# Expert layer: first-layer weights taken in alternating order, with loads cut into quarters and issued by the landing of earlier ones

## What is computed

```python
logits = einsum('bntd,des->bntes', grouped, Wc) + bc            # after a layernorm
perm = (logits + tie == max over the 32 tokens of a group)      # one token per expert and group
permuted = einsum('bnesd,...', grouped, perm)                   # gather
inner = relu(einsum('bnesd,esdf->bnesf', permuted, W1) + b1)    # 512 -> 32 per expert
result = einsum('bnesf,esdf->bnesd', inner, W2) + b2            # 32 -> 512 per expert
out = x + tanh(g_ffn) * einsum('bnesd,bntes->bntd', result, perm)   # scatter back
```

## Time and profile before

| | us |
|---|---|
| median of 3 runs | 1812.2 (1804.32 to 1812.33) |
| the profiled execution, its own time | 1815.87 |
| its span (first to last instruction) | 1814.1 |
| first gather of batch 0 | 754.5 |
| one batch, batches 1 to 14 | 62.1 to 67.7 |

### The profile page before, as it was taken

The page is one execution under the profiler, slowest core; times in us unless marked ns, Lnnn a source line. Parts: engine busy times, 40 slices in busy tenths (PEclk is TensorE's granted clock), DMA queues, the critical chain, the costliest instruction groups (busy, mean ns, idle before and its releaser), DMA issues.

```text
span 1814.1 us, 53065 instructions
## 1 busy us (share of the span) xinstructions
PE 1666.4 (92%) x23192; PEld 1178.4 (65%) x23192; DVE 1341.6 (74%) x1980; ACT 819.0 (45%) x1070; POOL 615.7 (34%) x841
## 2 busy tenths in 40 slices
PE   7899999999999999889999899999989999998974
PEld 3677777777777777767656656665765676576551
DVE  6877777777777777547777867877787787678657
ACT  3433333333333333465465555556546555554631
POOL 3577777777777777111011001101100110110100
PEclk9999999999999999999999999999999999999987
DMA  7345555545454544265667567567657766765762
GB/s 261 124 141 176 153 177 163 165 152 164 153 175 155 186 152 178 104 234 201 210 245 263 188 226 274 185 239 261 236 190 252 269 205 218 267 205 206 245 226 78
DMA packets 135845, 358.35 MB, mean 198 GB/s; under 512 B 13760, under 2 KB 17600, under 8 KB 117952
## 3 DMA queue, kind: packets, MB, share of 16 engines
q1 hardware_dynamic: 124384, 273.16, 45.0%
q10 hardware_dynamic: 11232, 81.79, 12.5%
HBM read 286.75 MB, written 68.16 MB: 196 GB/s over the span
## 4 chain that ended last, share of the span: by engine, by line
PE 57%; DVE 15%; issue 10%; POOL 10%; ACT 6%; DMA 1%; SPq 0%; POOLq 0%; DVEq 0%; ACTq 0%
PE ps L1220 14%; PE ps L1192 8%; PE ps L1247 8%; PE ps L208 6%; PE ps L836 6%; POOL qc L478 4%; POOL qc L479 4%; PE ps L1262 4%; PE ps L194 4%; PE ps L1242 3%; DVE mx L604 2%; DVE qc L620 2%; DVE qs L621 2%; ACT gat L1068 2%; PE ps L799 2%
## 5 line engine op out<-in xcount | busy, mean ns | idle before, releaser
L176 POOL TENSOR_TENSOR b_va<-b_mv,eps_layer 128x2 f32<-128x2 f32 x64 | 12.5, 195 | 858.3 <-DVE b_mv L167 857.3
L1108 DVE STREAM_TRANSPOSE res<-res 128x2048 f32<-128x2048 f32 x128 | 292.0, 2294 | 0.1
L1063 ACT ACTIVATE gat<-ps 128x1536 f32<-128x1536 f32 (+1 forms) x128 | 172.2, 1345 | 218.0 <-PE ps L1192 218.0
L779 PE MATMUL ps<-xTh,qh 128*128 128x512 f32 x512 | 208.9, 408 | 6.2 <-DVE qs L621 2.1
L779 PE MATMUL ps<-xTh,ql 128*128 128x512 f32 x512 | 200.0, 391 | 0.0
L779 PE MATMUL ps<-xTl,qh 128*128 128x512 f32 x512 | 200.0, 391 | 0.0
L1131 DVE COPY res<-ps 128x1024 f32<-128x1024 f32 x128 | 156.7, 1224 | 51.0 <-PE ps L1247 51.0
L1073 ACT ACTIVATE res<-ps 128x1024 f32<-128x1024 f32 x128 | 131.2, 1025 | 105.6 <-PE ps L1247 105.6
L1192 PE MATMUL ps<-sel,xin 32*128 32x128 f32 x4096 | 155.3, 286 | 25.1 <-ACT sel L236 13.6
L1192 PEld LDWEIGHTS ps<-sel,xin 32*128 32x128 f32 x4096 | 131.1, 188 | 61.1 <-ACT gat L1063 40.2
L1114 DVE COPY gat<-ps 128x512 f32<-128x512 f32 (+1 forms) x128 | 103.9, 812 | 84.2 <-PE ps L1192 83.9
(11 more groups left out here) (126 smaller groups left out, 3175.0 us busy)
## 6 DMA issues: line engine op xcount, KB each, us to landing
gat<-in_W ACTq DMA_DIRECT2D x48, 1024.0 KB, 7.8
xT<-in_xT SPq DMA_DIRECT2D x32, 1024.0 KB, 5.9
xin<-in_x SPq DMA_DIRECT2D x64, 512.0 KB, 3.8
x_scratch<-xin SPq DMA_DIRECT2D x64, 512.0 KB, 3.4
xin<-x_scratch SPq DMA_DIRECT2D x64, 512.0 KB, 4.2
xin<-x_scratch SPq DMA_DIRECT2D x128, 256.0 KB, 5.5
out<-xin SPq DMA_DIRECT2D x128, 256.0 KB, 3.6
xT<-in_W SPq DMA_DIRECT2D x25, 1024.0 KB, 5.2
```

What stands on the lines that cost most here:

```text
L779: last = e.matmul(ps[:, 2 + n % 2, :], a[:, c, n * DH:(n + 1) * DH], b[:, c, :], start=(k == 0), stop=(k == len(parts) - 1))
L1063: e.activation(o, v, ACT.Copy).then_inc(m_gaA.sem, 1)
L1108: e.transpose(v, v).then_inc(m_tr.sem, 1)
```

## The change

W1 is taken in order 0 to 7 in even batches and 7 to 0 in odd ones (`piece`). Pieces 2, 4, 5 stay on chip. The two pieces that a batch uses last lie in the two ring buffers and are the first two of the next batch, so a batch loads two ring pieces (`load_end`) and piece 3 (`load_middle`), which has the place of the y tiles 0 to 3: three pieces instead of five. Each is loaded as four quarters of 256 KB (2 KB for a partition) with a semaphore each, and a quarter is issued when the one two before it has landed. All W1 loads are SyncE's; ScalarE keeps the three W2 loads. `load_x` is cut into eight tiles of 256 KB, tile t issued when tile t-2 has landed and gather 6 or 7 is done. `load_y` 0 to 3 waits until `inner` has used the middle piece. The places of the relu's output and of W2's last piece change sides with the batch.

```diff
-W1_KEPT = (1, 4, 6)
-W1_MOVED = (0, 2, 3, 5, 7)
+W1_KEPT = (2, 4, 5)
+W1_MIDDLE = 3
+QUARTERS = 4
...
+        def piece(i, p):
+            return p if i % 2 == 0 else 2 * C - 1 - p
...
-            def load_x(i, v):
-                e.wait_ge(m_gap.sem, m_gap.at(i - 1, 2 * (C - 1) + v // 2))
-                e.wait_ge(m_w1.sem, m_w1.at(i - 1, 4 + v))
-                route.load(e, i, v)
+            def load_end(i, k, c):
+                e.wait_ge(m_w1.sem, m_w1.at(i, k))
+                if c >= 2:
+                    e.wait_ge(d_ring[k][c - 2].sem, d_ring[k][c - 2].at(i + 1))
+                e.dma_start(quarter(ring[k], c), quarter(w1_dram[piece(i, 2 * C - 1 - k)], c)).then_inc(d_ring[k][c].sem, 16)
+            def load_middle(i, c):
+                if i:
+                    k = (i - 1) * NT - NY + c
+                    e.wait_ge(d_ys[c].sem, d_ys[c].at(k // NY))
+                    e.wait_ge(m_w2.sem, m_w2.at(i - 1, 5))
+                if c >= 2:
+                    e.wait_ge(d_mid[c - 2].sem, d_mid[c - 2].at(max(i - 1, 0)))
+                e.dma_start(quarter(middle, c), quarter(w1_dram[W1_MIDDLE], c)).then_inc(d_mid[c].sem, 16)
+            def load_x(i, t):
+                e.wait_ge(m_gap.sem, m_gap.at(i - 1, 2 * (C - 1) + t // TH))
+                if t >= 2:
+                    e.wait_ge(route.d_x[t - 2].sem, route.d_x[t - 2].at(i))
+                route.load(e, i, t)
             def load_y(b, t):
                 k = b * NT + t
+                if t < NY and live(b + 1):
+                    e.wait_ge(m_w1.sem, m_w1.at(b + 1, piece(b + 1, W1_MIDDLE)))
...
             for i in range(B + 1):
+                if live(i):
+                    if i != 1:
+                        for c in range(QUARTERS):
+                            load_middle(i, c)
+                    for k, c in ((0, 0), (0, 1), (1, 0), (1, 1), (1, 2), (1, 3), (0, 2), (0, 3)):
+                        load_end(i, k, c)
+                for t in range(0, NY, 2):
+                    if live(i + 1):
+                        load_x(i + 1, t)
+                        load_x(i + 1, t + 1)
+                    if live(i - 1):
+                        load_y(i - 1, t)
+                        load_y(i - 1, t + 1)
+                for t in range(NY):
+                    if live(i + 1):
+                        load_x(i + 1, NY + t)
+                    if live(i - 1):
+                        store_y(i - 1, t)
                 if live(i - 1):
-                    for t in range(NY):
-                        load_y(i - 1, t)
-                if live(i):
-                    for m in (2, 3, 4):
-                        load_first(e, i, m)
-                if live(i + 1):
-                    for v in range(NV):
-                        load_x(i + 1, v)
-                if live(i - 1):
-                    for t in range(NY):
-                        store_y(i - 1, t)
                     for t in range(NY, NT):
                         load_y(i - 1, t)
                     for t in range(NY, NT):
...
-                    if u in (1, 4):
-                        load_first(e, i + 1, u // 3)
...
-            def inner(i, n):
-                c = n // 2
-                if n in W1_MOVED:
-                    k = NM * i + W1_MOVED.index(n)
-                    e.wait_ge(d_ring[k % 2].sem, d_ring[k % 2].at(k // 2))
+            def inner(i, p):
+                n, c = piece(i, p), p // 2
                 for q in range(n % 2 * 16, n % 2 * 16 + 16):
+                    if q % 4 == 0 and n not in W1_KEPT:
+                        e.wait_ge(*landed(i, p, q % 16 // 4))
```

More of the change, by code:

```diff
@@ L86, in build @@
         ring = [xT[:].rearrange("p c t -> p (c t)"), xin[:, 3].rearrange("p n d -> p (n d)")]
-        d_ring = [Mark(top, nc, f"ring{k}", 1, 16) for k in range(2)]
+        d_ring = [[Mark(top, nc, f"ring{k}{c}", 1, 16) for c in range(QUARTERS)] for k in range(2)]
         d_kept, m_b2s = Mark(top, nc, "kept", 1, 16), Mark(top, nc, "b2s")
@@ L147, in __init__ @@
         mark = lambda name, per=1, unit=1: Mark(top, nc, "b_" + name, per, unit)
-        self.d_x = [mark(f"x{v}", 1, 16) for v in range(NV)]
+        self.d_x = [mark(f"x{t}", 1, 16) for t in range(NT)]
         self.m_T, self.m_lg, self.m_sT = mark("T", NT), mark("lg", NT), mark("sT", 2)
@@ L404, in sync @@
                     e.wait_ge(d_o[0].sem, d_o[0].at(NU // RING - 1, 1))
-                    route.load(e, 0, 0)
-                    route.load(e, 0, 1)
+                    for t in range(4):
+                        route.load(e, 0, t)
                 if u == 29:
                     e.wait_ge(d_o[1].sem, d_o[1].at(NU // RING - 1, 1))
-                    route.load(e, 0, 2)
-                    route.load(e, 0, 3)
+                    for t in range(4, 8):
+                        route.load(e, 0, t)
                 if u in KEPT_AFTER:
@@ L952, in experts @@
         d_yl, d_ys = ([mark(f"{n}{k}", 1, 16) for k in range(NY)] for n in ("yl", "ys"))
+        d_mid = [mark(f"mid{c}", 1, 16) for c in range(QUARTERS)]
         d_room = {u: mark(f"room{u}", 1, 16) for u in W2_MOVED}
@@ L961, in experts, with first, landed, second @@
         bank = lambda u: 4 - u % 2 * 4
-        NM = len(W1_MOVED)
-        def first(i, n):
+        middle = y.rearrange("p n d -> p (n d)")
+        def piece(i, p):
+            return p if i % 2 == 0 else 2 * C - 1 - p
+        def first(i, p):
+            n = piece(i, p)
             if n in W1_KEPT:
                 return kept[:, W1_KEPT.index(n), :]
-            return ring[(NM * i + W1_MOVED.index(n)) % 2]
-        def second(u):
+            return middle if n == W1_MIDDLE else ring[p % 2 if p < 2 else 1 - p % 2]
+        def landed(i, p, c):
+            n = piece(i, p)
+            if n == W1_MIDDLE:
+                return d_mid[c].sem, d_mid[c].at(max(i - 1, 0))
+            d = d_ring[p % 2 if p < 2 else 1 - p % 2][c]
+            return d.sem, d.at(i if p < 2 else i + 1)
+        def second(i, u):
             if u in W2_KEPT:
@@ L1080, in scalar @@
                             route.chosen(e, i, 1)
-                    for h in range(2):
+                    for p in (2 * C - 2, 2 * C - 1):
                         for j in range(4):
-                            hidden(i, j, h)
+                            hidden(i, j, p)
                 if live(i + 1):
```

66 lines of the change are left out of this document (33 added, 33 removed).

## The result

| | before | after |
|---|---|---|
| median | 1812.3 us (1804.32 to 1813.15) | 1844.1 us (1839.89 to 1848.89) |
| the profiled execution, its own time | 1815.87 | 1848.89 |
| its span | 1814.1 | 1847.1 |

The change makes the kernel slower: after / before is 1.019, 95% interval 1.015 to 1.022. The forecast of 1808.8 us and its range, which ended at 1832, are both missed.

What follows compares the result with a forecast made beforehand. TensorE was taken as the bound, busy 1666 of 1814 us, stalled by instruction fetches queued behind 1 MB loads. From 1815.9, -23.5 - 3.3 + 22.4 + 1.0 gives 1812.5; the median lies 3.7 lower, so 1808.8 us, range 1784 to 1832.

Steps and rivals of the forecast that it cites:

- Fewer and smaller W1 loads: First layer: instruction fetches queue behind 512 KB of quarters instead of whole 1 MB loads, so TensorE's stalls shrink; gain 23.5 us.
- the upper bound of 1.0: First layer: most stall time left, the longest stall of 2.1 us less 1.1, once a batch.
- the 0.6 taken: First layer: stalls taken as left, some 1.7 late fetches of 0.35 us each, 0.6 us a batch.
- Token loads 5 to 7 behind the stores: Scatter and routing: tile 7 lands late beside the first W2 load, delaying turn 6 by 1.6 us in 14 batches, +22.4 us.
- The 6.1 us to landing: Routing: time taken for token tile 7 to land once issued beside the first W2 load, instead of 2.7 to 2.8.
- The upper bound (2.6 us a batch): Routing: greatest lateness of turn 6, if token tile 7 takes 7.1 us to land.
- I take that as covered: Second layer: store 3 and y tiles 4 to 7 behind tile 7 delay `finish` 4 to 7, assumed to cost nothing.
- rival 2: Second layer: y tile 7 lands late, so `finish` 7 delays it about 1.5 us in 14 batches; +21, 1830 us; chance 0.18.
- The second layer: Second layer: one middle piece replaces two W1 loads and four y tiles, so its two gaps vanish; gain 3.3 us.
- The start: First batch: eight quarters in a row could hold one instruction fetch; +1 us (0 to 2.1).
- The other waits on TensorE and SyncE: Some 15 more TensorE waits a batch and new SyncE list waits cost nothing; bounds 0.75 us a batch, 3 us an odd batch.
- The rule that spoke against the first term: First layer: engines alternate between queues by packet, so fetches wait one packet; if right, gains would be 0, the sum +23.4.

Runs made afterwards that it cites:

- e3: The changed kernel with all eight token tiles ahead of the y stores and each W1 piece loaded whole instead of in quarters: 1839.1 us.
- e4: The changed kernel with all eight token tiles ahead of the y stores and W1 quarters not waiting for the one two before: 1835.2 us.
- e14: The kernel before with 50 one-column copies on ScalarE ahead of the normalisation of token tile 6, making turn 6 late: 1867.3 us.
- e13: The kernel before with 35 one-column copies on ScalarE ahead of the normalisation of token tile 6, making turn 6 late: 1833.9 us.
- the four copies runs: The kernel before with 17, 24, 35 or 50 one-column copies on ScalarE ahead of the normalisation of token tile 6: 1805.2, 1817.2, 1833.9, 1867.3 us.
- e7: The kernel before with moving W1 pieces loaded once and never reloaded, so its output is not the reference's: 1767.8 us.
- e6: The changed kernel with the three W2 loads issued after turns 3, 5 and 7 instead of 1, 3 and 5: 1792.4 us.
- e8: The changed kernel with token tiles ahead of the stores, each behind a first-layer piece, not waiting for the tile two before: 1798.1 us.
- e5: The changed kernel with the token loads of the kernel before, four of 512 KB, all ahead of the stores: 1801.2 us.

## Why the prediction was wrong

**Fewer and smaller W1 loads: the size right by luck, the reason wrong.** Forecast -23.5, measured -23.4. But the step said that 2 MB less are worth nothing alone and that what lies ahead of a fetch, 512 KB or 1 MB, decides. e3 and e4 speak against both: quarters and pacing show no gain, which leaves the missing load. Nor is the sum made as it was put. The gaps in batches 1 to 15 fell by 17.4 us (31.1 to 13.6, those under "issue" at gather and first layer together); the other 6.0 us are 12 us at half clock, four stretches in which the clock fell in the first layer of before and none after. One of the four, in batch 6 (columns as above):

```profile
1161.30:1164.70 3.40, 3.40 (x63) 3.06 (x58) 0.89 (x2) 0.89 (x1) 0.00 (x0) 0.50 0.42 154
```

The gaps that are left are 0.9 us a batch, near the upper bound of 1.0, not the 0.6 taken; they were to be under 1 us each, and go up to 2.4.

**Token loads 5 to 7 behind the stores: the step that failed, by its size.** Place, chain and time of issue were right: tile 7 at the first W2 load, 2.6 us from landing to `normed`. The term was 14 x 1.6 = 22.4 us; the stretch lost 49.4. Three parts of it:
- Turn 6 was late by 29.6 us in sum and turn 7 by 0.9 more. The 6.1 us to landing came from tiles during whose flight SyncE's queue moved 0.8 to 1.3 MB; here it was 1.0 to 1.5 MB, and landing took 7.5 us on average in the 11 late batches. The upper bound (2.6 us a batch) was passed in four of them, since 7.1 us was taken as the worst landing and tile 7 needed up to 8.4.
- The clock: in six batches turn 7 came 4.05 to 4.62 us behind turn 6 instead of 2.42, 10.4 us in sum. No step had this; e14 shows the price with nothing else changed, and e13 that the 1.6 us of the forecast would not have paid it.
- `outer` 0 waited for `finish` 7, 8.1 us in three gaps (batches 8, 12 and 14). "I take that as covered" was wrong, and rival 2 named it; it came in the batches where turn 6 was on time.

Together 29.6 + 0.9 + 10.4 + 8.1 = 49.0 of the 49.4; small terms of both signs make the rest. The forecast and rival 2 had been put as alternatives; they were one cause with two payers.

**The second layer.** The gaps at its products are gone, as forecast. Forecast -3.3, measured -2.3 over batches 1 to 14, the 8.1 us aside, which are reckoned above because they stand ahead of L1290, from where this stretch is counted. The wait for `finish` 7 has a second price here: in batches 12 and 14 the clock fell to half behind it, and the second layer took 14.5 and 14.7 us, where it took 12.2 to 12.3 in the other batches. These 4.8 us belong to the failed step, too. That the stretch still came out shorter is because before lost 4.0 us there besides its two gaps, which no run explains. Behind the gap of batch 12 (columns as above):

```profile
1600.90:1607.30 6.40, 6.33 (x92) 1.73 (x108) 3.96 (x5) 1.76 (x2) 0.00 (x0) 0.50 0.14 46
```

**The start.** Forecast +1. The first gather came 2.5 us later, but not by the change: in the four copies runs and e7, whose first 750 us are those of before, it came at 756.6 to 757.1. Batch 0 took 5.7 us more, with 5.1 us of gaps at the first layer against 2.5 and 10.2 us at half clock against 3.4. With the same start it took 59.8 us in e6, 60.0 in e8 and 62.5 in e5, so I claim no cause for it.

**The other waits on TensorE and SyncE** cost nothing, as forecast: e5, which has them all, has a scatter stretch of 20.65 us.

**The rule that spoke against the first term.** The Trainium skill, page "DMA: Bandwidth & Descriptors", section "Queues, rings and completion order", has each DMA engine take turns between the queues that have work, by which quarters would gain nothing. I set it aside for one fetch that started as the load ended; 19 of the 27 late ones did. What it says of quarters came out (16.1 against 17.1 us). That two busy queues share the engines is also what the two data queues show, which moved 1.32 and 1.34 MB beside each other, though in 722 and 180 packets of the profile, so that turns by these packets are not shown. Had I used that much on tile 7, I would have halved SyncE's queue for as long as the W2 load runs. It does not explain why a fetch is late at all beside a W1 load, and e7 shows that it is; what holds it stays open.

## What to carry to other kernels

A small load at the end of an in-order list pays for what else goes over its queue, and here twice that beside a big load on another queue (a 256 KB tile: 2.8 us with 0.8 MB going over its queue, 4.0 with 1.1 MB, 8.0 with 1.3 MB beside a W2 load): look at what is issued in the microseconds before a critical landing, and move the big load that has slack (here two turns, 52 us). Where two things on one list are both critical, their order decides which engine waits (e3); give the list less to wait for, here by dropping the wait for earlier landings. And a late step on TensorE can cost more than its own length: look at the granted clock behind the gap, too.

## What the hardware showed beyond expectation

The granted clock of TensorE falls to half behind some of the gaps and takes part of the gain or loss of a stall with it: 6.0 us of the first layer's gain and 10.4 us of the routing's loss were clock, not waiting. It is no simple matter of the gap: the same 2.68 us in the same place brought it in nine batches of 14. Two DMA queues with work shared the engines by bytes rather than packets (1.34 and 1.32 MB in the 8.0 us of batch 10, although one counted 180 packets and the other 722; in the 11 late batches SyncE's queue moved 1.0 to 1.5 MB beside 1.0 to 1.35 MB of the W2 loads).
